# Token preparation, logits, threshold search and slot chain inside the shared network, as one unrolled program of 64 steps

## The reference

```
h = tok(x)                       # stride-2 convolution + mean + layer norm: (32, 188, 256), T = 6016 tokens
h = h + attn(layernorm(h))       # 16 heads, decay on the scores, latent k and v
n = layernorm(h)                 # flat_x, 6016 x 256
scores = softmax(n @ gate_w.T).T # 16 experts x 6016 tokens
topk_weight, topk_idx = top_k(scores, 752)          # per expert
eo = (gelu(xg @ Wg.T) * (xg @ Wu.T)) @ Wd.T * topk_weight   # xg = flat_x[topk_idx]
out = h + scatter_add(eo) + (gelu(n @ Sg.T) * (n @ Su.T)) @ Sd.T   # the last term is the shared network
```

## Time and profile before

| | |
|---|---|
| median of three runs | 2146.38 us (2142.93 to 2149.76) |
| the profiled execution: its time, its span | 2143.69 us, 2141.9 us |
| busy, share of the span | PE 82%, PEld 60%, DVE 57%, ACT 42%, POOL 44% |
| chain that ended last, by engine | issue 33%, PE 20%, POOL 18%, DMA 12%, DVE 10%, SPq 3% |
| mean granted TensorE clock | 0.913 of full speed |

### The profile page before, as it was taken

One profiled execution on the slowest core, in us unless ns is written; L12 is line 12 of the kernel. 1 busy time (PEld: TensorE's weight loads), 2 busy tenths in 40 slices (PEclk: granted clock), 3 DMA queues, 4 the chain that ended last, 5 costly groups with the idle time before them and its releaser, 6 DMA issues.

```text
span 2141.9 us, 48763 instructions
## 1 busy us (share of the span) xinstructions
PE 1763.1 (82%) x15898; PEld 1280.2 (60%) x15898; DVE 1230.0 (57%) x3696; ACT 908.1 (42%) x1862; POOL 943.2 (44%) x921
## 2 busy tenths in 40 slices
PE   6957899999999845439999238999999999999997
PEld 5844566666666524327777235666666666666665
DVE  3875788888888843315555664444444444444442
ACT  3534556666666531113332144444444444444442
POOL 3851344444444320002222014666666666666666
PEclk9987999999999975559999558999999999999999
DMA  5614555555555511110000023333333333333312
GB/s 167 205 33 88 119 127 131 126 129 129 129 127 129 115 51 39 46 45 22 29 29 29 15 82 131 88 90 89 88 88 88 88 88 88 88 88 88 88 27 29
DMA packets 211857, 186.32 MB, mean 87 GB/s; under 512 B 157136, under 2 KB 192464, under 8 KB 205648
## 3 DMA queue, kind: packets, MB, share of 16 engines
q1 hardware_dynamic: 184912, 141.12, 24.8%
q0 software_dynamic: 26880, 44.36, 9.6%
HBM read 134.51 MB, written 50.44 MB: 86 GB/s over the span
## 4 chain that ended last, share of the span: by engine, by line
issue 33%; PE 20%; POOL 18%; DMA 12%; DVE 10%; SPq 3%; ACT 1%; POOLq 1%; DVEq 1%; PEld 0%; ACTq 0%; PEldq 0%
POOL arena L573 7%; DMA score_table<-arena 4%; DMA out<-hidden,arena 4%; POOL arena L599 4%; PE psum L1520 3%; POOL out L608 3%; DVE arena L981 3%; DVE psum L989 2%; PE psum L1360 2%; PE psum L1303 2%; PE psum L1257 2%; SPq L416 2%; PE psum L1325 2%; PE psum L1271 2%; PE psum L1537 1%
## 5 line engine op out<-in xcount | busy, mean ns | idle before, releaser
L573 POOL TENSOR_TENSOR arena<-arena 128x376 f16<-128x376 f32 x320 | 348.5, 1179 | 580.2 <-ACT arena L644 563.9
L1520 PE MATMUL psum<-arena,hidden 128*128 128x376 f16 x3072 | 503.2, 323 | 42.4 <-DVE arena L1192 41.5
L1520 PEld LDWEIGHTS psum<-arena,hidden 128*128 128x128 f16 x3072 | 296.5, 98 | 244.9 <-DVE arena L1192 62.8
L644 ACT ACTIVATE arena<-arena 128x376 f16<-128x376 f32 (+5 forms) x610 | 287.5, 474 | 59.4 <-DVE arena L1192 53.6
L1192 DVE SCALAR_TENSOR_TENSOR arena<-psum,arena 128x376 f32<-128x376 f32 x256 | 140.1, 547 | 281.3 <-ACT arena L821 186.9
L821 ACT ACTIVATE arena<-psum 128x376 f32<-128x376 f32 x256 | 123.7, 483 | 401.4 <-PE psum L1520 395.6
L981 DVE CUSTOM_DVE_ANT_0 arena<-psum,constants 128x188 f32<-128x188 f32 x768 | 227.9, 345 | 108.4 <-PE psum L1257 107.3
L644 ACT ACTIVATE arena<-psum 128x188 f32<-128x188 f32 (+8 forms) x467 | 173.8, 400 | 259.8 <-PE psum L1409 46.4
L1537 PE MATMUL psum<-hidden,arena 128*128 128x256 f16 (+1 forms) x2304 | 256.7, 273 | 15.3 <-POOL arena L573 15.3
L1537 PEld LDWEIGHTS psum<-hidden,arena 128*128 128x128 f16 (+1 forms) x2304 | 229.0, 103 | 39.8 <-POOL arena L573 18.4
L693 ACT ACTIVATE arena<-psum 128x564 f32<-128x564 f32 x256 | 164.0, 641 | 103.8 <-PE psum L1271 102.2
(11 more groups left out here) (153 smaller groups left out, 2798.6 us busy)
## 6 DMA issues: line engine op xcount, KB each, us to landing
arena<-q_halves SPq DMA_DIRECT2D x384, 47.0 KB, 2.5
arena<-k_halves SPq DMA_DIRECT2D x384, 47.0 KB, 2.2
arena<-e_g SPq DMA_DIRECT2D x16, 1024.0 KB, 5.0
arena<-e_u SPq DMA_DIRECT2D x16, 1024.0 KB, 5.4
arena<-e_d SPq DMA_DIRECT2D x16, 1024.0 KB, 5.1
arena<-x_t SPq DMA_DIRECT2D x32, 376.0 KB, 3.5
weighed<-arena POOLq DMA_DIRECT2D x32, 376.0 KB, 4.0
token_table<-arena SPq DMA_DIRECT2D x8, 799.0 KB
```

Of the source, the lines that this page charges most:

```text
L573: nc.gpsimd.tensor_tensor(dst, f, hi, ALU.subtract).then_inc(ready, 1)
L644: return nc.scalar.activation(dst, src, ACT.Copy, scale=scale)
L1520: last = mm(bank[2 * (s % 2) + i][:, 0:CHUNK], w_, a, start=n == 0, stop=n == 5)
```

## The change

Stages 2, 3 and 4 become one straight program of `STEPS` = 64 steps `s = 4k + m` on every engine, one step for each chunk `k` and hidden block `m`, without loops, without the barriers between them.

- Rows: `XR`, a ring of four buffers of one batch (2 tiles), takes the place of `ROWS`. VectorE normalises even batches, GpSimd odd ones; each waits for the transfer of the batch four before (`row_out`). Steps 0 to 13 normalise two batches each (4+2s, 5+2s), steps 0 to 14 turn two batches each (2s+2, 2s+3).
- Transfers: every batch's rows are written by a transfer of their own (`rows_out`, 32 of them), the scores of 16 tiles by another (`scores_out`, 4 of them, 64 bytes for each token), the turned scores by two for each 16 tiles (`turned_scores_out`). `SC8` is loaded after the last of them, at SyncE's step 20.
- Logits: computed turned, experts on partitions, four chunks at once in four groups of 32 partitions (`turned_logits`, 24 matmuls of 376 columns for each 16 tiles), then turned back. This takes the place of 384 matmuls of 16 columns.
- Down products: chunks 0 to 4 whole at block 1 of the next chunk, from chunk 5 on one tile in each step, five steps behind.
- Search: 30 rounds instead of 32, one in each step; VectorE counts for the first time in step 23 (`FIRST`), TensorE sums in steps 24 to 53. The slot chain follows, a part in each of steps 53 to 60.
- The storage of the one-hot stage's operands moves; the stage's instructions do not change.

```diff
+KS = T // CHUNK
+STEPS = 4 * KS
+PREP = 15
+WHOLE = 5
+QUADS = 4
+FIRST = 23
+ROUNDS = 30
...
+        prep = at3.at
+        XR = [at3(2 * D) for _ in range(RING)]
+        PSC = at3(TILES * E)
...
+        def normal_rows(eng, tensor_scalar, b):
+
+            if b >= RING:
+                eng.wait_ge(rt_done, b - RING + 1)
+                eng.wait_ge(row_out[b % RING], 16 * (b // RING))
+            for qt in range(2):
+                t = 2 * b + qt
+                last = tensor_scalar(XR[b % RING][0:HT, qt * D:(qt + 1) * D], H[0:HT, t, :], MV[0:HT, t, 0:1],
+                                     RSTD[0:HT, t, :], ALU.subtract, ALU.mult)
+            last.then_inc(row_ready[b % 2], 1)
...
+            def rows_out(b):
+                sp.wait_ge(row_ready[b % 2], b // 2 + 1)
+                sp.dma_start(xtab[b * S:(b + 1) * S, 0:D].rearrange("(t p) n -> p t n", p=HT),
+                             XR[b % RING][0:HT, :].rearrange("p (t n) -> p t n", t=2)).then_inc(row_out[b % RING], 16)
+
+            def scores_out(q):
+                sp.wait_ge(score_ready, q + 1)
+                sp.dma_start(xtab[q * 16 * HT:(q + 1) * 16 * HT, D:ROW].rearrange("(t p) n -> p t n", p=HT),
+                             PSC[0:HT, q * 16 * E:(q + 1) * 16 * E].rearrange("p (t n) -> p t n", n=E)).then_inc(score_out, 16)
+
+            def turned_scores_out(q):
+                sp.wait_ge(sct_ready, q + 1)
+                for h in range(2):
+                    sp.dma_start(sctab[:, (2 * q + h) * CH:(2 * q + h + 1) * CH].rearrange("e (t n) -> t e n", n=HT),
+                                 SCT[q % 2][:, h * HT:(h + 1) * HT]).then_inc(sct_out[q % 2], 16)
+
+            def chunk_out(k):
+                sp.wait_ge(sh_added, 2 * k + 2)
+                sp.dma_start(out[k * CHUNK:(k + 1) * CHUNK, :].rearrange("(t p) n -> p t n", p=HT),
+                             SOUT[k % 2][0:HT, :].rearrange("p (t n) -> p t n", t=4)).then_inc(sh_out[k % 2], 16)
+
+            for b in range(RING):
+                rows_out(b)
+            for s in range(STEPS):
+                k, m = divmod(s, 4)
+                if RING + 2 * s < B:
+                    rows_out(RING + 2 * s)
+                    rows_out(RING + 2 * s + 1)
+                if m == 2 and 1 <= k <= QUADS:
+                    scores_out(k - 1)
+                if m == 0 and 2 <= k <= QUADS + 1:
+                    turned_scores_out(k - 2)
+                if s == 4 * QUADS + 4:
+                    for par in range(2):
+                        sp.wait_ge(sct_out[par], 32 * QUADS // 2)
+                    sp.dma_start(SC8, sctab[:, :].rearrange("e (c n) -> (e c) n", c=8)).then_inc(sc8_in, 16)
+                if m == 3 and 1 <= k <= WHOLE:
+                    chunk_out(k - 1)
+                if m == 2 and k >= WHOLE + 2:
+                    chunk_out(k - 2)
+            for k in range(KS - 2, KS):
...
+            for s in range(STEPS):
+                k, m = divmod(s, 4)
+                if RING + 2 * s < B:
+                    normal_rows(pool, nc.gpsimd.tensor_scalar, RING + 2 * s + 1)
+                c = slice(m * CHUNK, (m + 1) * CHUNK)
+                low_hidden(SHL[k % 2][:, c], SHF[m], SHH[k % 2][:, c], hh_ready, s + 1, hl_ready)
+                if s == FIRST:
+                    pool.wait_ge(rt_done, B)
+                    for i in range(RING):
+                        pool.wait_ge(row_out[i], 16 * (B // RING))
+                    pool.wait_ge(score_out, 16 * QUADS)
+                    for par in range(2):
+                        pool.wait_ge(sct_out[par], 32 * QUADS // 2)
+                    nc.gpsimd.memset(ONE, 1.0).then_inc(ones_ready, 1)
...
+            high_rows(0)
+            high_rows(1)
+            for s in range(STEPS):
+                k, m = divmod(s, 4)
+                act.wait_ge(gu_done, s + 1)
+                if s >= 2:
+                    act.wait_ge(hf_ready, s - 1)
+                nc.scalar.activation(SGEL[s % 2], bank[2 * (s % 2)][:, 0:CHUNK], ACT.Gelu, scale=1.0 / WSCALE).then_inc(gel_ready, 1)
+                if s < PREP:
+                    high_rows(2 * s + 2)
+                if m == 1 and 1 <= k <= QUADS:
+                    act.wait_ge(lsub_done, k)
+                    v = PSC[0:HT, (k - 1) * 16 * E:k * 16 * E]
+                    nc.scalar.activation(v, v, ACT.Exp, scale=1.0 / WSCALE).then_inc(lexp_done, 1)
+                act.wait_ge(hf_ready, s + 1)
+                if m == 0 and k >= 2:
+                    act.wait_ge(down_done, 4 * k - 4)
+                copy(SHH[k % 2][:, m * CHUNK:(m + 1) * CHUNK], SHF[m]).then_inc(hh_ready, 1)
+                if s < PREP:
+                    high_rows(2 * s + 3)
...
+            done = FIRST + ROUNDS
+            for s in range(STEPS):
+                k, m = divmod(s, 4)
+                dve.wait_ge(gel_ready, s + 1)
+                if s >= RING:
+                    dve.wait_ge(hl_ready, s - RING + 1)
+                nc.vector.scalar_tensor_tensor(SHF[m], bank[2 * (s % 2) + 1][:, 0:CHUNK], HSCALE / WSCALE, SGEL[s % 2],
+                                               ALU.mult, ALU.mult).then_inc(hf_ready, 1)
+                if s < PREP:
+                    low_rows(2 * s + 2)
+                if RING + 2 * s < B:
+                    normal_rows(dve, nc.vector.tensor_scalar, RING + 2 * s)
+                if s < PREP:
+                    low_rows(2 * s + 3)
+                if FIRST < s <= done:
+                    decide(s - FIRST - 1)
+                if FIRST <= s < done:
+                    count(s - FIRST)
+                if m == 2 and 1 <= k <= WHOLE:
+                    down_out(k - 1, 0)
+                    down_out(k - 1, 1)
+                if m == 3 and k > WHOLE:
+                    down_out(k - 1, 0)
+                if m == 1 and k > WHOLE + 1:
+                    down_out(k - 2, 1)
...
+            def turn_rows(b):
+                pe.wait_ge(row_ready[b % 2], b // 2 + 1)
+                if b >= 2:
+                    pe.wait_ge(rtl_ready, b - 1)
+                for c in range(2):
+                    for qt in range(2):
+                        last = nc.tensor.transpose(bank[6 + b % 2][:, c * S + qt * HT:c * S + (qt + 1) * HT],
+                                                   XR[b % RING][0:HT, qt * D + c * 128:qt * D + (c + 1) * 128], ident[0:HT, 0:HT])
+                last.then_inc(rt_done, 1)
...
+            def down(n_):
+                k, i, u = n_ // 4, n_ // 2 % 2, n_ % 2
+                if i + u == 0:
+                    pe.wait_ge(hl_ready, 4 * k + 4)
+                if u == 0 and k >= 1:
+                    pe.wait_ge(sh_added, 2 * k + i - 1)
+                if u == 0 and i == 1 and k < QUADS:
+                    pe.wait_ge(lsub_done, k + 1)
+                if u == 0 and i == 1 and k == QUADS:
+                    pe.wait_ge(sct_ready, QUADS)
+                n = 0
...
+            def turned_logits(q):
+                pe.wait_ge(rtl_ready, 8 * q + 8)
+                if q >= 1:
+                    pe.wait_ge(sh_added, 2 * q - 1)
+                n = 0
+                for c in range(2):
+                    w = slice(W_GATE + c * E, W_GATE + c * E + 32)
+                    for low_w, low_x in ((False, False), (True, False), (False, True)):
+                        for g in range(4):
+                            last = mm(bank[4][32 * g:32 * g + 32, 0:CHUNK], (WL if low_w else WH)[:, w],
+                                      (TOKL if low_x else TOKH)[:, 4 * q + g, c, :], start=n == 0, stop=n == 5)
+                        n += 1
                 last.then_inc(lg_done, 1)
...
+            turn_rows(0)
+            turn_rows(1)
+            done = FIRST + ROUNDS
+            for s in range(STEPS):
+                k, m = divmod(s, 4)
+                if m == 0:
+                    pe.wait_ge(rtl_ready, 2 * k + 2)
+                if s >= 2:
+                    pe.wait_ge(hf_ready, s - 1)
+                gate_up(k, m)
+                if s < PREP:
+                    turn_rows(2 * s + 2)
+                    turn_rows(2 * s + 3)
+                if m == 0 and 1 <= k <= QUADS:
+                    logits_back(k - 1)
+                if m == 3 and 1 <= k <= QUADS:
+                    turn_scores(k - 1)
+                if m == 3 and k < QUADS:
+                    turned_logits(k)
+                if m == 1 and 1 <= k <= WHOLE:
+                    for i in range(4):
+                        down(4 * k - 4 + i)
+                if s >= 4 * WHOLE + 5:
+                    down(s - 5)
+                if FIRST < s <= done:
+                    pe.wait_ge(count_ready, s - FIRST)
+                    mm(bank[7][:, 0:1], C[:, C_ONES:C_ONES + 128], COUNT, start=True, stop=True).then_inc(total_done, 1)
...
+            for n_ in range(STEPS - 5, STEPS):
+                down(n_)
```

More of the change, by code:

```diff
@@ L1011, in _ @@
             meet(dve)
-            dve.sem_inc(rtl_ready, 2)
-            for par in range(2):
```

(36 more changed lines are left out.)

412 lines of the change are left out of this document (167 added, 245 removed).

## The result

| | before | after |
|---|---|---|
| median, device us | 2144.65 (2141.53 to 2149.76, 4 runs) | 2091.03 (2089.99 to 2091.68, 4 runs) |
| profiled execution: its time, its span | 2143.69, 2141.9 | 2089.99, 2088.2 |
| rows first normalised, one-hot stage begins | 798.18, 1212.80 | 799.79, 1160.99 |
| mean granted TensorE clock | 0.913 | 0.929 |

After over before is 0.9747, with a 95% interval of 0.9726 to 0.9768: faster by 53.6 us. The two profiled executions place it. Token preparation, network and slot chain took 414.6 us and now take 361.2, 53.4 less; the stages in front end 1.6 us later, the stages behind take 1.9 less; together 53.7, the difference of the spans.

A forecast was written before the change was run, and what follows sets the result against it. Two DMA engines bound stage 2, TensorE stage 3, waits stage 4. 212.6 us on the pair, then 140 of TensorE, start the one-hot stage at 1160.2, not 1212.8: -52.6, so 2091.1; plus 2.7, 2094 us; range 2060 to 2150.

The forecast's parts named there:

- The pair of DMA engines: Before the search's first count: rows 140.8, outputs 32.1, turned scores 3.6, scores 36.1 us pass two DMA engines; sum 212.6.
- The one price that no row had: Score writes: a 64-byte packet was taken at 12 ns, making 9.0 us a transfer, 36.1 us for four.
- The lower end: Score writes: 6 ns for a small packet, from the first loads' row; it takes 18 us off.
- Both rivals on small packets: Score writes: packets cost by bytes, 2063 to 2088 us (0.24), or like large ones, 2184 us (0.13 beyond 29.5 ns).
- The pair does not pause: Preparation: four row buffers hold 17.6 us of DMA work, covering TensorE's longest step, 15.8 us, and the other engines.
- TensorE meanwhile: Preparation: TensorE, at half clock, reaches the first sum at 987 us and waits 32 us for the scores.
- From there on TensorE: After the first count: TensorE's remaining work takes 140 us, VectorE's 3.2 us a step hides; one-hot stage begins at 1160.2.
- Rival 3: Search steps 0.3 us longer, or the DMA pair pausing in preparation: 10 to 30 us, 2104 to 2124 us; chance 0.17.
- Nothing for the slot chain: After the search: the slot chain's vector work, 2 us a step, hides beside TensorE's steps.
- Rival 4: Preparation: transfers share no pair, so it follows TensorE, 1979 us; outputs alone elsewhere 2062 us; chance 0.05.
- the rule on divisors: Table and output transfers: engines are the largest number up to 16 dividing the slowest dimension; 94 partitions give two.

## Why the prediction was right

Forecast 2094 us in 2060 to 2150; measured 2091.0. By the profiled execution 2091.1 against 2090.0. The steps, one by one:

- **The pair of DMA engines: right, in the sum and in the terms.** Load of `SC8` usable at 1017.9 us forecast (its own terms, 1014.6 and 3.1, add to 1017.7), 1018.5 measured. Rows 4.4 us each, measured 4.43; outputs 8.0, measured 7.8; scores 9.0, measured 8.3 in the trace and 8.9 by the kernel that writes them twice. The one price that no row had, 12 ns for 64 bytes, is 11 to 11.8. That the number came so near is luck: it was picked between 6 and 42, not worked out. The lower end, 6 ns from the earlier trace rows, was half of what is measured, and it hangs on a small difference: the prediction set 6.4 us for the packets (0.4 us of sixteen engines) where the row's 111.2% makes 7.1, and with 7.1 the 98 small packets cost 13 ns. Each ns is 3.0 us of the forecast, so 6 ns would have given 2076 us. Both rivals on small packets fall with the measured price. By the Trainium skill (same page as above, section Why small descriptors are slow (HBM only)) I had put an estimate of 6 ns beside it, from its beats and cycles; the measured 11 to 11.8 ns is nearly twice that.
- **The pair does not pause: right.** None of forty slices is empty. Chunk 3 was added 19 us before the turn of its output came (974.17 and 993.21), so the queue always had its next transfer. The 9.0 us that VectorE waited for an output buffer at 997.03 were for chunk 4, whose output stands behind the load of `SC8`; the prediction does not name this wait, and it held up nothing that the load needed. That one pair serves all these transfers, the reason that the prediction gives for adding them up, is not shown apart from the order of the one queue (see the kernel with the rows alone cut): both give this sum.
- **TensorE meanwhile: right in the result, not in the picture.** It reached the first sum at 990.8 us (987 forecast) and waited 29.0 us (32). But I had it at half clock in all of the preparation, and the granted clock was 0.69 to 0.79 there: in each whole down product it rose, in the waits it fell. GpSimd's row operation took 1.21 us, just above the bound of 1.2 that I gave it. Both were hidden by the pair.
- **From there on TensorE: right.** 140 us forecast; 1019.77 to 1160.27 is 140.5. Steps of 3.36 us, so VectorE's 3.2 us did fit; with the first count in step 26 its work is the same in each step and fits as well. Rival 3 (VectorE or starts and stops bind) falls.
- **Nothing for the slot chain: right.** 16.4 us of it are hidden.
- **Rival 4, transfers that do not share a pair**, was wrong about this kernel and near in its price: 1979 us forecast, 1970.9 once the partitions are cut so that they divide. What was tried is more engines for each transfer, not different pairs; by the issue held in the kernel with the rows alone cut, different pairs in one queue might have brought less.
- **What the prediction did not see.** It named two DMA engines as the bound of stage 2 and worked it out to the microsecond, and weighed the change only against that. Its rows and the rule on divisors beside them were enough to ask what the old kernel gives with the transfers cut at 80 partitions: 63 us, more than the change.

## To carry to other kernels

When a stretch moves at one flat rate that is a small fraction of the queue's, look at the count of partitions of its transfers and divide its share of sixteen engines out: 94 partitions ran on two engines, 47 on one, 80 and 14 on nearly all by their rates, and cutting the transfers cost a few lines. Add up the work of such a bottleneck in the order of its queue, whichever engines each transfer has, for every transfer before the first one that an engine needs, small packets by their number and not their bytes; that sum gave the end of the wait within 1 us. Overlapping compute with a transfer queue that is already full gains only the compute time: first free the queue, then fuse.

## What the runs showed of the hardware

- A packet of 64 bytes from on-chip memory to a DRAM table took 11 to 12 ns of its engine; one of 1 KB 42 to 47 ns. Smaller is cheaper, but sixteen times fewer bytes cost only four times less.
- An issue on SyncE's queue took 0.24 to 0.5 us where the transfers kept up (and most of those of the kernel cut at 80) and 4.43 us where they did not: SyncE itself is held back at the rate of the transfers, so that later issues, the outputs too, stand behind it. A row issue with sixteen engines was held 6.88 us by a score write on two.
- Two halves of 47 partitions each, issued one right behind the other, gave 22 GB/s together, the rate of one engine.
- TensorE's granted clock followed its pauses: 0.69 to 0.79 between 797 and 950 us with 89.3 of 153 us busy, 0.92 and then 1.00 with 142.6 busy once the transfers were cut. That a queue which holds TensorE up thus costs twice is argued, not measured: here the pair covered the slower clock.
